# Set-up of a fused attention, S4D and expert kernel: time steps computed in two columns, bias rows and four loads moved to ScalarE, set-up slots redone

## The reference

```python
dt = jnp.exp(log_dt)                       # 256 values, one per channel
A = A_re + 1j * A_im                       # 256 x 64
dtA = dt[:, None] * A
dC = C * (jnp.exp(dtA) - 1.0) / A
K = 2.0 * jnp.einsum('dn,dnl->dl', dC, jnp.exp(dtA[:, :, None] * jnp.arange(L))).real
```

## Time and profile before

| | |
|---|---|
| median of 3 runs | 1806.69 us (1806.36 to 1807.74) |
| profiled execution | 1804.41 us, of which the span is 1802.6 us |
| DVE busy | 1479.2 us (82%), PE 78%, POOL 67%, ACT 62% |
| chain that ended last | DVE 52%, PE 15%, POOL 12%, issue 11%, ACT 7%, DMA 3% |

### The profile page before, as it was taken

One profiled execution on the slowest core, in us unless ns is written; L12 is line 12 of the kernel. 1 busy time (PEld: TensorE's weight loads), 2 busy tenths in 40 slices (PEclk: granted clock), 3 DMA queues, 4 the chain that ended last, 5 costly groups with the idle time before them and its releaser, 6 DMA issues.

```text
span 1802.6 us, 20762 instructions
## 1 busy us (share of the span) xinstructions
PE 1409.9 (78%) x6269; PEld 987.7 (55%) x6269; DVE 1479.2 (82%) x2091; ACT 1111.9 (62%) x2366; POOL 1204.7 (67%) x1349
## 2 busy tenths in 40 slices
PE   6566658778876878679878878897788778878796
PEld 3233445455544555547565646564656465655796
DVE  7999999999999999889998999899989993103121
ACT  3689844856485648555976587658864775233442
POOL 1499838577856885697678958895789568515232
PEclk8666778879887988799999999898989989988898
DMA  7200120012102200122232222232223210843232
GB/s 214 59 5 2 39 68 31 24 45 56 25 12 49 50 24 7 47 83 76 76 83 65 73 72 71 62 88 74 59 65 87 55 53 22 266 121 105 62 51 27
DMA packets 96451, 115.16 MB, mean 64 GB/s; under 512 B 17840, under 2 KB 73144, under 8 KB 96196
## 3 DMA queue, kind: packets, MB, share of 16 engines
q1 hardware_dynamic: 84196, 99.26, 19.0%
q0 software_dynamic: 12144, 14.58, 5.1%
HBM read 75.48 MB, written 19.58 MB: 53 GB/s over the span
## 4 chain that ended last, share of the span: by engine, by line
DVE 52%; PE 15%; POOL 12%; issue 11%; ACT 7%; DMA 3%; SPq 1%; POOLq 0%; DVEq 0%
DVE R L1419 18%; DVE ZB L1422 15%; DVE ZB L1415 6%; DVE R L1411 6%; PE PS L1952 3%; DVE R L1376 2%; DMA out<-R 2%; ACT ZB L1009 2%; POOL ZB L725 2%; POOL R L904 2%; ACT R L1015 2%; PE PS L2063 2%; POOL R L898 1%; POOL xs_d L882 1%; PE PS L1971 1%
## 5 line engine op out<-in xcount | busy, mean ns | idle before, releaser
L1419 DVE MAX8 R<-ZB 128x8 f32<-128x1024 f32 x384 | 471.3, 1227 | 12.2
L1422 DVE MATCH_REPLACE8 ZB<-R,ZB 128x1024 f32<-128x1024 f32 x384 | 464.1, 1209 | 0.0
L1012 ACT ACTIVATE R<-PS 128x512 f32<-128x512 f32 (+6 forms) x412 | 181.8, 470 | 193.6 <-PE PS L2017 32.2
L725 POOL TENSOR_TENSOR ZB<-ZB 128x1024 f32<-128x1024 f32 x96 | 231.6, 2413 | 94.6 <-ACT ZB L1009 90.8
L727 POOL TENSOR_TENSOR ZB<-ZB 128x1024 f32<-128x1024 f32 x96 | 226.5, 2359 | 7.5
L1009 ACT ACTIVATE R<-R 128x32 f32<-128x32 f32 (+4 forms) x356 | 96.4, 275 | 196.9 <-DVE R L1419 172.1
L1411 DVE MAX8 R<-PS 128x8 f32<-128x1024 f32 x128 | 156.2, 1220 | 1.2 <-PE PS L1705 1.2
L1415 DVE MATCH_REPLACE8 ZB<-R,PS 128x1024 f32<-128x1024 f32 x128 | 155.4, 1214 | 0.0
L1015 ACT ACTIVATE R<-R 128x1 f32<-128x1 f32 (+1 forms) x384 | 140.7, 391 | 20.2 <-POOL R L712 15.2
L1009 ACT ACTIVATE ZB<-ZB,R 128x1024 f32<-128x1024 f32 x128 | 146.2, 1143 | 0.3 <-DVE ZB L1422 0.2
L1009 ACT ACTIVATE ZB<-PS,R 128x1024 f32<-128x1024 f32 x128 | 142.6, 1114 | 4.2
(11 more groups left out here) (247 smaller groups left out, 3048.1 us busy)
## 6 DMA issues: line engine op xcount, KB each, us to landing
ZR<-ZR SPq DMA_DIRECT2D x96, 128.0 KB
ZB<-in_L_ffn_rt_gate SPq DMA_DIRECT2D x21, 512.0 KB, 4.1
ZB<-in_L_ffn_rt_up SPq DMA_DIRECT2D x21, 512.0 KB, 5.0
ZB<-in_L_ffn_rt_down SPq DMA_DIRECT2D x21, 512.0 KB, 6.3
R<-in_x SPq DMA_DIRECT2D x16, 512.0 KB, 4.9
ZB<-in_ctx SPq DMA_DIRECT2D x8, 768.0 KB, 5.4
R<-xs_d SPq DMA_DIRECT2D x39, 128.5 KB, 2.2
out<-R SPq DMA_DIRECT2D x32, 128.0 KB, 1.7
```

Of the source, the lines that this page charges most:

```text
L725: pool.tensor_tensor(e, e, w, ALU.subtract).then_inc(s.g_att, 1)
L1012: return act.activation(o, i, ACT.Copy, **k)
L1419: vec.max(ml[:, 8 * r:8 * r + 8], w).then_inc(s.v_tk, 1)
L1422: vec.match_replace(w, ml[:, 8 * r:8 * r + 8], w, NEG).then_inc(s.v_tk, 1)
```

## The change

Four edits:

1. **Time steps.** log_dt is loaded as two columns of 128 (256 values, one value a partition and chunk) early in SP's queue, in place of the broadcast to 128 x 256. DVE computes `exp` on 128 x 2 (the same 17 instructions) right behind the moments of x, and scales the identity by each column (`diag`, 128 x 128, twice). PE multiplies an all-ones matrix by `diag` (two matmuls, behind the transposes of A and C), which lays dt out in rows in PSUM bank 0; DVE reads dt from there in its two products. The scores of tile 0, which use that bank, wait for it.
2. **FiLM bias rows** go from DVE (4 TENSOR_SCALAR of 1 x 256) to ACT (4 ACTIVATE of 1 x 256), right behind the last FiLM weight copy; POOL's `weights` and PE's FiLM matmuls wait for ACT's semaphore instead.
3. **The eight loads of A and C** are issued by ACT as its first instructions instead of SP.
4. **Slots.** About thirty tables of the set-up, of `prep` and of the chunks have new numbers. Those of `prep`, keys and SP's moves hold for every batch.

```diff
@@ sync
                 sp.dma_start(ident, a["c_id"]).then_inc(s.ld_id, 16)
+                sp.dma_start(dtc[:, 0:2], a["L0_xattn_log_dt"].rearrange("(c p) -> p c", p=128),
+                             allow_slow_non_contiguous=True).then_inc(s.ld_dt, 16)
                 sp.dma_start(cb[0], cr[0]).then_inc(s.c_in0, 16)
...
-                for k, nm in enumerate(("A_re", "A_im", "C_re", "C_im")):
-                    for dup in range(2):
-                        sp.dma_start(adx[:, k, :, dup * 64:dup * 64 + 64],
-                                     a["L0_xattn_" + nm].rearrange("(c p) n -> p c n", p=128)).then_inc(s.ld_a, 16)
-                sp.dma_start(ldt, row2(a["L0_xattn_log_dt"], 256)).then_inc(s.ld_dt, 16)
@@ gpsimd weights
-                on.wait_ge(s.v_w, 2)
+                on.wait_ge(s.a_row, 2)
@@ scalar
+            def kernel_inputs():
+                yield -90
+                for k, nm in enumerate(("A_re", "A_im", "C_re", "C_im")):
+                    for dup in range(2):
+                        act.dma_start(adx[:, k, :, dup * 64:dup * 64 + 64],
+                                      a["L0_xattn_" + nm].rearrange("(c p) n -> p c n", p=128)).then_inc(s.ld_a, 16)
@@ scalar weights
+                yield ACT_ROW[0]
+                on.wait_ge(s.ld_wb, 32)
+                on.wait_ge(s.ld_cst, 16)
+                for half in range(2):
+                    w_scale, w_shift = (wvf2[64:65, half * 512 + lo:half * 512 + lo + 256] for lo in (0, 256))
+                    affine(w_scale, w_scale, scale=mgc[64:65, :], bias=C["jj"][64:65, 1:2]).then_inc(s.a_row, 1)
+                    copy(w_shift, w_shift, scale=mgc[64:65, :]).then_inc(s.a_row, 1)
@@ vector kernel_rows
+                yield prep_at(0) + 0.1
+                on.wait_ge(s.ld_dt, 16)
+                expm1(dtc[:, 2:4], dtc[:, 0:2], 2)
+                chain(TS, dtc[:, 2:4], dtc[:, 2:4], 1.0, None, ALU.add)
+                on.wait_ge(s.ld_id, 16)
+                for c in range(2):
+                    chain_to(s.v_dt, TS, diag[:, c, :], ident, dtc[:, 2 + c:3 + c], None, ALU.mult)
                 yield DVE_RAY[0]
...
-                on.wait_ge(s.ld_dt, 16)
                 on.wait_ge(s.ld_cst, 16)
-                expm1(dt, ldt)
-                chain(TS, dt, dt, 1.0, None, ALU.add)
-                chain(TT, aR, dt, are, ALU.mult)
-                chain(TT, th, dt, aim, ALU.mult)
+                on.wait_ge(s.p_dt, 1)
+                chain(TT, th, dtp, aim, ALU.mult)
+                TT(aR, dtp, are, ALU.mult).then_inc(s.v_dt, 1)
                 yield DVE_RAY[1]
-                expm1(e1, aR)
+                on.wait_ge(s.v_dt, 3)
+                expm1(e1, aR, 256)
@@ tensor attention
+                    if n == 0:
+                        on.wait_ge(s.v_dt, 3)
@@ tensor kernel_rows, behind the transposes of A and C
+                on.wait_ge(s.v_dt, 2)
+                for c in range(2):
+                    ins = pe.matmul(dtp[:, 128 * c:128 * c + 128], ones, diag[:, c, :], start=True, stop=True)
+                ins.then_inc(s.p_dt, 1)
```

The slots that matter most below, old and new. PE's order at the start changes from context, A/C transposes, first-half keys to context, first-half keys, A/C transposes:

```diff
-PE_PREP = (4, 8.2, 11.8, 14.8, 14.8, 21.6, 39.1, 39.2, 40.3)
+PE_PREP = (3.7, 5.2, 9.8, 15.2, 15.5, 22.8, 38.8, 38.8, 42.2)
-PE_WEIGHT = (-35.6, -14.3, 5.3, 5.7, 9, 12.9)
+PE_WEIGHT = (-32.7, -25.4, 3.3, 6.4, 8.2, 12.9)
-PE_RAY = (-65.7, -21.2, -12.8)
+PE_RAY = (-62.7, -28.6, -26.3)
-DVE_WEIGHT = (-42.9,)
+DVE_WEIGHT = (-2.1,)
-ACT_WEIGHT = (4.3, 6.2, 11.9, 19.2, 22.9)
+ACT_WEIGHT = (2.6, 5.8, 10.4, 11.7, 17.9)
+ACT_ROW = (18.4,)
-SP_QUERY = (-13.1, -13.1, -6.1, -3.6)
+SP_QUERY = (-19.9, -17.7, -13.7, -10.2)
-SP_KEYS = (-20.6, -20.3, -27.7, -23.5)
+SP_KEYS = (-16.5, -22.8, -30.8, -38.7)
-ACT_VALUE = ((-10.3, 23.9, 26.8), ...
+ACT_VALUE = ((5.7, 20.8, 24.1), ...
```

More of the change, by code:

```diff
@@ L139 @@
 POOL_SH = ((133.7, 135.1, 136.1, 143), (141.9, 147, 148, 148.3))
-POOL_PREP = (7.7, 98.3)
-POOL_LOW = (17.6, 23.7, 48.6)
+POOL_PREP = (8.2, 101)
+POOL_LOW = (17.8, 22.7, 48.1)
 ACT_FILM_IN = ((19.4, 22.2, 27.2, 27.5), (19, 19.9, 24.8, 29.6))
@@ L157 @@
 DVE_ROUTE = ((118.3, 119.4), (123.3, 123.3))
[L158 to L161, removed]
+ACT_PREP = (14.5, 16.8, 17.7)
+ACT_QUERY = (21.8, 21.8, 25.3)
+ACT_CONTEXT = (8.3, 43.7)
+ACT_KEY = (15.2, 57.2)
 ACT_FINISH = ((-0.2, 0.4, 3.9, 21.7), (8.7, 9.6, 14.8, 23.5), (0.7, 7, 16.8, 29.3), (-2, -2, 6.2, 17.5))
@@ L202 @@
[L202 to L211, removed]
+ACT_MOMENTS = (5.3, 12.5)
+PE_WEIGHT = (-32.7, -25.4, 3.3, 6.4, 8.2, 12.9)
+ACT_WEIGHT = (2.6, 5.8, 10.4, 11.7, 17.9)
+DVE_WEIGHT = (-2.1,)
+POOL_WEIGHT = (9,)
+DVE_RAY = (-61.6, -61, -60.4)
+ACT_RAY = (-21.6, -18.1, -18.1)
+PE_RAY = (-62.7, -28.6, -26.3)
@@ new lines @@
+ACT_VALUE = ((5.7, 20.8, 24.1), (24.2, 36.5, 36.8), (39, 42.5, 49.9), (53.8, 66.6, 70.9), (71.1, 74, 76.6), (76.9, 87.4,
+             89.8), (89.9, 98.4, 98.6), (99.6, 121.2, 121.2))
+POOL_CHUNK = ((-27, -27, -10.5, -10.5), (-23.6, -10.5, 14.5, 18.1), (-10.5, 1.7, 30.3, 34.3), (26.1, 29.1, 57.1, 58.6), (44.1,
+              53.3, 62.8, 63.9), (62.3, 62.3, 65.6, 77), (64.6, 65.6, 81.2, 86.5), (79.2, 80.7, 94.2, 103.1))
+SP_CHUNK = (-37.2, -23.9, -22.6, 19.7, 19.7, 36.2, 52.6, 74, 77)
+SP_LATE = (-47.9, 119)
@@ L212 @@
+PE_END = (113.6, 121.2, 121.2, 121.2, 125.5, 125.5)
+ACT_END = (122, 126, 126.4, 127.1, 128.2, 130.1)
+DVE_END = (124.8, 127.6, 130.7, 132.9, 134.5, 137.3)
+ACT_ROW = (18.4,)
 T_TURN, T_GATE, T_UP, T_DOWN = range(4)
@@ L1365, in routed @@
                     act.activation(acts[j % 3], PS[:, 1, :], ACT.Silu).then_inc(s.a_silu, 1)
-            weave(attention(), finish(), prep(), keys(), weights(), kernel_rows(), kernel_values(), post(), shared(), tiles(), routed())
+            weave(kernel_inputs(), attention(), finish(), prep(), keys(), weights(), kernel_rows(), kernel_values(), post(), shared(), tiles(), routed())
         @block.vector
@@ L1433, in weights @@
                 TT(b1c, q_bank("weight", 0, 0)[:, 0:8], b1l, ALU.add).then_inc(q_sem("weight", 0, 0), 1)
[L1434 to L1444, removed]
-                chain(STT, rr, c1, -LN2_HI, x, ALU.mult, ALU.add)
-                chain(STT, rr, c1, -LN2_LO, rr, ALU.mult, ALU.add)
-                cs = [1.0 / float(np.prod(np.arange(1.0, k + 1))) for k in range(1, 9)]
-                chain(TS, c2, rr, cs[7], None, ALU.mult)
-                for k in range(6, -1, -1):
-                    chain(STT, c2, c2, cs[k], rr, ALU.add, ALU.mult)
-                chain(TS, c3.bitcast(I32), c1, 127.0, 8388608.0, ALU.add, ALU.mult)
-                chain(TT, c2, c2, c3, ALU.mult)
-                chain(STT, o, c3, -1.0, c2, ALU.add, ALU.add)
+            def expm1(o, x, n):
+                k1, k2, k3, r = (v[:, 0:n] for v in (c1, c2, c3, rr))
+                chain(TS, k1, x, LOG2E, MAGIC, ALU.mult, ALU.add)
+                chain(TS, k1, k1, -MAGIC, -126.0, ALU.add, ALU.max)
+                chain(TS, k1, k1, 127.0, None, ALU.min)
+                chain(STT, r, k1, -LN2_HI, x, ALU.mult, ALU.add)
+                chain(STT, r, k1, -LN2_LO, r, ALU.mult, ALU.add)
+                cs = [1.0 / float(np.prod(np.arange(1.0, k + 1))) for k in range(1, 9)]
+                chain(TS, k2, r, cs[7], None, ALU.mult)
+                for m in range(6, -1, -1):
+                    chain(STT, k2, k2, cs[m], r, ALU.add, ALU.mult)
+                chain(TS, k3.bitcast(I32), k1, 127.0, 8388608.0, ALU.add, ALU.mult)
+                chain(TT, k2, k2, k3, ALU.mult)
+                chain(STT, o, k3, -1.0, k2, ALU.add, ALU.add)
```

20 lines of the change are left out of this document (9 added, 11 removed).

## The result

The changed kernel takes 1804.15 us (median of 22 runs, 1800.83 to 1808.16), the kernel before 1806.62 us on the same chip (22 runs, 1802.5 to 1809.95). The ratio is 0.9985, 95% interval 0.9978 to 0.9992: 2.7 us faster, 1.4 to 4.0. The forecast was a gain of 7.7 us, outside that interval. The profiled executions stand 1.9 us apart (1802.48 against 1804.41 us, spans 1800.7 and 1802.6).

What follows compares the result with a forecast made beforehand. DVE bounds the kernel, as a queue of attention tiles from the first MAX8. An earlier first MAX8 gains 8.0 us, less 0.3 lost is 7.7: median 1806.69 - 7.7 = 1799.0 us, range 1794.8 to 1803.2.

Steps and rivals of the forecast that it cites:

- Bounds and place: Attention tiles queue at DVE from the first MAX8 at 59.48 us; starting it earlier moves the whole kernel.
- Time steps: DVE set-up: 17 wide instructions, 8.0 us, leave the chain; narrow ones take 3.4 us, hidden in the wait for A and C.
- PE's order and the chain: Set-up: keys precede A and C transposes on PE, so only 4.0 - d us are kept; DVE's chain ends at 48.1 + d.
- d: Set-up: time by which the context lands later than before; taken as 1.4 us, ends 0 and 2.5.
- What is late next: Set-up: PE's angle becomes the limit by 0.6 us; first MAX8 at 51.45, a gain of 8.0 us.
- Bias rows: DVE set-up: 6.1 us leave DVE; the four instructions cost ACT 1.9 us.
- ACT and POOL follow: First tiles: POOL's slack for tile 2 shrinks from 4.0 to about 1 us or less; a loss of 0.3 us counted.
- Slots that hold for every batch: Frames: ACT and POOL orders change little, SP's change is only a risk, otherwise nothing; no cost counted.
- Rival 1: Set-up: earlier start partly given back by late context, narrow chain or POOL; 3.7 to 6 us remain, about 1801.8; chance 0.18.
- Rival 2: Up to batch 1: ACT and POOL set the pace, DVE waits 8 us more; no change, about 1806; chance 0.07.
- Rival 3: Frame ends: fourth expert tile's down weights, about 7.5 us later behind key moves, stall PE; slower, about 1812; chance 0.04.
- Rival 4: Set-up and first tiles: context not late, most of DVE's 4.6 us idle taken; gain 10 to 13 us, about 1795.5; chance 0.11.

Runs made afterwards that it cites:

- k1_ac_sp: k1_first with the eight loads of A and C issued by SP behind Wk, as in the kernel before: 1797.39 us, ratio 0.9954.
- rows_on_dve_b: k1_ac_sp with the four bias-row scalings back on DVE behind the bias column, none on ACT: 1802.48 us, ratio 0.9981.
- k1_first: Changed kernel with PE's second key product at slot 40.3 again from batch 1 on, ahead of tile 3's down product: 1799.49 us, ratio 0.9964.
- k1_ac_sp_early: k1_ac_sp with PE's transposes of A and C ahead of the first-half keys: 1797.18 us, ratio 0.9954.
- sp_moves_old: Changed kernel with SP's slots of queries, keys and inputs as in the kernel before from batch 1 on: 1802.64 us, ratio 0.9982.
- before_k1_late: Kernel before with PE's second key product at slot 42.2 from batch 1 on, behind tile 3's down product: 1808.91 us, ratio 1.0020.
- dt_behind_b: k1_first with the narrow time-step load behind the context's load on SP's queue, A and C still by ACT: 1797.41 us, ratio 0.9960.
- early_rays_b: k1_ac_sp_early with PE's ray transposes ahead of the 32 one-column products and ACT's ray copies earlier: 1799.27 us, ratio 0.9957.

## Why the prediction was wrong

*Bounds and place.* Right. What starts the queue at DVE earlier moves the kernel: k1_ac_sp, with a lead of 9.1 us at the first MAX8, is 8.3 us faster (0.0046 x 1806.6, interval 5.6 to 11.0).

*Time steps.* Right: 17 narrow instructions in 3.3 us (3.4 forecast), hidden, done at 12.7. The wide ones that they replace were 8.0 us in the trace of before; put back behind the new front they are 7.1. The two scaled identities cost 0.24 each, for which I took 0.3.

*PE's order and the chain.* Right to a few tenths: transposes at 18.19 (from 18.5 + d less their own 1.94, 18.0), copies ended at 21.0 (20.7), chain ended at 49.76 (49.5).

*What is late next.* The limit did not pass to PE. The angle started at 48.49 and its rounding followed DVE's chain without a gap (49.68). I had the angle later, at 49.1, a wait of DVE in front of the rounding, and the first MAX8 at 51.45; it came at 50.88, with no wait. Moving A and C forward shows where that limit is: DVE's chain then ends 4.2 us earlier, at 45.6, and waits 2.73 us for the angle.

*Bias rows.* 6.1 us forecast for this term, 4.9 to 5.1 measured (rows_on_dve_b).

*d, the context's delay.* Mis-sized. I took 1.4 from bytes and rate; the one profile of the changed kernel says 1.43, and by that alone the step would pass. Five kernels with this front say 1.4 to 4.3 over 9.56, mean 2.8. The order of the loads counted as well as their bytes, which I did not weigh: the narrow load stands right ahead of the context. Taking one of the two edits back gave 0.7 to 1.8 us over k1_first (0.9960 and 0.9954 against 0.9964; the intervals overlap). The Trainium skill (Trainium Kernel Development and Optimization, Key Constraints) says that the queues share the engines. The prediction's estimate by that rule, near 2.5, is nearer to the mean than my 1.4. The runs with ACT's loads and no narrow one ahead (0.3 and 0.6 over 9.96) agree with it less.

*ACT and POOL follow.* Right: the distance at tile 15 is 8.3 of 8.6, a loss of 0.3 as forecast.

*The end of the set-up.* Not in the sum: 2.2 us are lost at tiles 16 to 19 in this pair, 1.5 in k1_first, 2.1 in k1_ac_sp, 0.5 in k1_ac_sp_early, none in sp_moves_old. PE idles 13.2 us there, waiting for DVE, in all of them. Afterwards its clock comes back at different times; 16 products of 128x256 take 5.70 us after and 3.70 before:

```profile
227.87 1.94 PE L1872 MATMUL PS<-R 128*128 128x128 f32 x8 [13.20 <-DVE R L1542]
...
233.57 5.70 PE L1889 MATMUL PS<-R 128*128 128x256 f32 x16 [0.94 <-DVE R L1548]
```

```profile
236.14 1.94 PE L1852 MATMUL PS<-R 128*128 128x128 f32 x8 [13.24 <-DVE R L1528]
...
241.51 3.70 PE L1869 MATMUL PS<-R 128*128 128x256 f32 x16 [1.17 <-DVE R L1534]
```

The size of the loss goes with how long PE's clock stays low behind that idle time. In the 12 us behind it the granted clock is 0.60 after, 0.85 before and 0.85 in sp_moves_old. Of the fourteen traces, the seven with 0.80 or more lose 0.9 us or less against before, the seven with 0.50 to 0.64 lose 1.5 to 2.2. No experiment was made on it; that the clock wanders there between executions and is no property of the change is only a reading of these traces.

*Slots that hold for every batch: "Orders on ACT and POOL change little. SP's change is the risk below; otherwise nothing."* This is the step that failed. I weighed SP, ACT and POOL and left PE out, though `PE_PREP[8]` had its old and new values in the diff on either side of the down product. The term that I put at nothing costs 3.8 us by the ratio of k1_first and 3.6 by that of before_k1_late (intervals 1.1 to 6.5 and 2.0 to 5.2), and 5.0 and 5.1 us in the profiles of the changed kernel and before_k1_late. The forecast 7.7 less 3.7 for K1 and less 1.0 to 1.4 for d, which is its mean delay of 2.4 or 2.8 less my 1.4, gives 2.6 to 3.0, and 2.7 was measured. That this closes to a tenth is partly luck: the sum leaves out the loss at the end of the set-up, the first MAX8 that came earlier than forecast, and a last stretch that differs between executions. In the one pair of profiles the account is 8.6 at the first MAX8, less 0.3 to tile 15, 2.2 to tile 19, 0.8 to tile 75, 5.0 at the three frame ends and 1.1 at tile 127, and 2.7 given back at the end: 1.9.

*Rivals.* The time lies between rivals 1 and 2, and the gain of 2.7 us is below the 3.6 that the prediction itself wanted before it called a change faster. Rival 1 (1801.8) had one of its causes, the late context. Rival 2 (1806) had the nearer time and not its mechanism: ACT and POOL kept up, and DVE's idle time from the first MAX8 to that of tile 16 is 5.0 us where it was 4.5. Rival 3, the down weights behind the key moves, did not happen: with SP's old moves the time is the same (0.9982 against 0.9985). Its rows belong to the last expert tile of the frame, which is the fifth there and not the fourth. After the change those weights are issued at 944.87 instead of 942.04, not 7.5 us later, and PE takes them at 953.44 without a wait. Rival 4 needed a context on time. My last paragraph said that a distance that changes from frame to frame would show the sum wrong; it does, and in that view the cause can be seen.

Five kernels have an interval below that of the changed kernel: k1_first, and beyond it k1_ac_sp (1797.39), k1_ac_sp_early (1797.18), dt_behind_b (1797.41) and early_rays_b (1799.27). The last four, of five or six runs each, cannot be told from each other; each is 7 to 8.3 us faster than before by its ratio, which is what the forecast had wanted of the change.

## What to carry to other kernels

When a change rewrites slots that a loop shares, list for every engine the pairs whose order flips, PE's among them, and ask of each what the instruction now in front waits for. If no other work fills that wait, it is paid in every frame that has the pair, and with it whatever PE's clock loses. Then compare the kernels by their distance at a recurring instruction; a set-up gain of 8.6 us and a loss of 1.6 to 1.9 us at each of three frame ends look like a small gain in the totals and like two plain facts in that table. And one profile of a front is one draw: a load time that agreed with the forecast to 0.03 us was the best of five.
